# A pairwise-interaction tower: 31 couples of products added ahead of the sums, by GpSimd and by accumulating DMAs, with a longer ring and lag

## What is computed

```python
e = stack([tbl_f[ids[:, f]] for f in range(40)], axis=1)      # 512 x 40 x 64
viW = einsum('bpd,pde->bpe', e[:, i_idx, :], W)                # W: 780 x 64 x 64
z = einsum('bpe,bpe->bp', viW, e[:, j_idx, :])                 # 512 x 780
h = concatenate([z, dense_ctx], axis=1)                        # 512 x 796
h = maximum(h @ W_top1 + b_top1, 0)                            # 512
h = maximum(h @ W_top2 + b_top2, 0)                            # 256
y = h @ W_top3                                                 # 1
```

## Time and profile before

| | us |
|---|---|
| median of three runs | 349.21 |
| the profiled execution's own time | 349.04 |
| its span, first to last instruction | 346.9 |
| TensorE matmuls, busy | 329.1 (95%) |
| VectorE, busy | 249.6 (72%) |
| GpSimd, busy | 225.6 (65%) |
| ScalarE, busy | 22.1 (6%) |

### The profile page before, as it was taken

The page is one execution under the profiler, slowest core; times in us unless marked ns, Lnnn a source line. Parts: engine busy times, 40 slices in busy tenths (PEclk is TensorE's granted clock), DMA queues, the critical chain, the costliest instruction groups (busy, mean ns, idle before and its releaser), DMA issues.

```text
span 346.9 us, 4306 instructions
## 1 busy us (share of the span) xinstructions
PE 329.1 (95%) x1676; PEld 115.1 (33%) x1676; DVE 249.6 (72%) x248; ACT 22.1 (6%) x35; POOL 225.6 (65%) x191
## 2 busy tenths in 40 slices
PE   0799979899999999999999999999999999999997
PEld 0133333233333333333333333333333333333442
DVE  2484968778787888978889888988888898840000
ACT  1001100000000000000001000010000000000032
POOL 6777777777778889877788788576887423520000
PEclk9999989999999999999999999999999999999999
DMA  6984443243423238731322323232110000000000
GB/s 167 255 231 146 119 106 105 81 102 91 115 57 104 64 96 261 170 104 33 96 85 62 89 68 86 62 69 85 39 23 2 0 3 0 0 2 0 0 2 0
DMA packets 17854, 27.59 MB, mean 80 GB/s; under 512 B 4901, under 2 KB 5029, under 8 KB 17834
## 3 DMA queue, kind: packets, MB, share of 16 engines
q1 hardware_dynamic: 9770, 17.86, 17.7%
q0 software_dynamic: 4608, 4.73, 6.9%
q10 hardware_dynamic: 3456, 4.72, 4.8%
HBM read 22.57 MB, written 0.00 MB: 65 GB/s over the span
## 4 chain that ended last, share of the span: by engine, by line
PE 80%; POOL 13%; issue 4%; DMA 1%; ACT 0%
PE ps_t L421 47%; PE ps_z L443 21%; POOL rows L265 13%; PE ps_t L465 5%; PE ps_e L404 2%; PE ps_t L488 2%; PE ps_e L465 2%; DMA rows<-in_tbl,ids_sb 1%; DMA ids_sb<-in_ids_t 1%; PE ps_t L494 1%; ACT y_sb L328 0%
## 5 line engine op out<-in xcount | busy, mean ns | idle before, releaser
L372 DVE TENSOR_TENSOR prod<-ps_t,E 128x1024 f32<-128x1024 f32 x200 | 231.7, 1217 | 45.7 <-PE ps_t L421 44.9
L421 PE MATMUL ps_t<-E,w_sb 64*128 64x512 f32 x800 | 189.8, 609 | 0.8 <-ACT E L294 0.7
L265 POOL DMA_INDIRECT rows<-in_tbl,ids_sb x144 | 137.8, 957 | 43.4 <-issue 41.9
L272 POOL TENSOR_TENSOR prod<-prod 128x1024 f32<-128x1024 f32 x37 | 86.8, 2370 | 37.4 <-DVE prod L372 37.3
L421 PEld LDWEIGHTS ps_t<-E,w_sb 64*128 64x128 f32 x800 | 71.1, 187 | 109.6 <-issue 82.2
L443 PE MATMUL ps_z<-prod,quads 128*32 128x512 f32 x572 | 76.8, 600 | 0.0
L443 PEld LDWEIGHTS ps_z<-prod,quads 128*32 128x32 f32 x572 | 15.1, 109 | 48.9 <-DVE prod L372 29.1
L351 DVE TENSOR_SCALAR prod<-prod,first_row_f 125x512 f32<-125x512 int32 x38 | 16.6, 495 | 11.1 <-PE ps_e L395 5.1
L294 ACT ACTIVATE E<-ps_e 128x512 f32<-128x512 f32 x18 | 10.8, 598 | 192.4 <-PE ps_e L404 171.1
L395 PE MATMUL ps_e<-prod 125*64 125x512 f32 x40 | 12.1, 694 | 11.2 <-DVE prod L351 10.0
L465 PE MATMUL ps_t<-z,w_sb 128*128 128x512 f32 (+1 forms) x42 | 18.6, 595 | 0.0
(11 more groups left out here) (26 smaller groups left out, 21.1 us busy)
## 6 DMA issues: line engine op xcount, KB each, us to landing
w_sb<-in_w_units SPq DMA_DIRECT2D x50, 256.0 KB, 2.9
E<-E ACTq DMA_DIRECT2D x72, 64.0 KB, 2.3
rows<-in_tbl,ids_sb POOLq DMA_INDIRECT x144, 2.6
w_sb<-in_w SPq DMA_DIRECT2D x7, 256.0 KB, 4.5
prod<-in_ids_by_field SPq DMA_DIRECT2D x2, 512.0 KB, 9.0
prod<-in_tbl SPq DMA_DIRECT2D x3, 312.5 KB
w_sb<-in_w SPq DMA_DIRECT2D x1, 512.0 KB, 7.1
prod<-in_tbl SPq DMA_DIRECT2D x1, 250.0 KB
```

What stands on the lines that cost most here:

```text
L265: pool.indirect_dma_start(rows[:, g % G_RING, b, f * DIM:(f + 1) * DIM], None, tables[2 * k + f], bass.IndirectOffsetOnAxis(ap=ids_sb[:, c ...
L272: pool.tensor_tensor(prod[:, n % P_RING, 0, :, :], prod[:, n % P_RING, 0, :, :], prod[:, n % P_RING, 1, :, :], ALU.add).then_inc(halves_ad ...
L372: dve.tensor_tensor(prod[:, n % P_RING, s, :, :], ps_t[:, (2 * n + s) % STEPS, :, :], multiplier, ALU.mult).then_inc(product_ready, 1)
L421: last = pe.matmul(ps_t[:, step % STEPS, j, :], w_sb[at:at + DIM, m % W_RING, col:col + P], E[at:at + DIM, slot_of(pairs_of(n)[s][j]), :], ...
```

## The change

Three sizes change, the list of added groups is written out per couple, and half of the additions are made by DMAs that GpSimd issues. In the string a letter stands for each couple: P, GpSimd adds the halves of both groups itself; D, GpSimd issues for each of the two groups a DMA that adds the second half onto the first (`accum_op`); a dot, the couple is reduced in full. There are 15 P couples and 16 D couples.

```diff
-W_RING = 12
-P_RING = 8
+W_RING = 8
+P_RING = 12
-LAG = 7
+LAG = 11
-ADDED = [n for n, (_, M) in enumerate(GROUPS) if M is not None and n >= 20 and n // 2 % 2 == 1]
+ADDER = "........DPDP.PD.D.DPDP...DPPDPP.DPD.DPD..DPDPDPDP."
+ADDED_BY_POOL = [n for n in range(NG) if ADDER[n // 2] == "P"]
+ADDED_BY_DMA = [n for n in range(NG) if ADDER[n // 2] == "D"]
+ADDED = sorted(ADDED_BY_POOL + ADDED_BY_DMA)
-        E4 = sb("E4", [P, QUADS, 2, BATCH])
+        E4 = sb("E4", [P, QUADS - 1, 2, BATCH])
+        halves_added_by_dma = [sem(f"halves_added_by_dma{i}") for i in range(P_RING)]
             def add_halves(n):
                 pool.wait_ge(product_ready, 2 * n + 2)
+                if n in ADDED_BY_DMA:
+                    pool.dma_start(prod[:, n % P_RING, 0, :, :], prod[:, n % P_RING, 1, :, :],
+                                   accum_op=ALU.add).then_inc(halves_added_by_dma[n % P_RING], 16)
+                    return
                 pool.tensor_tensor(...)
...
                 for g in (n, n + 1):
                     pe.wait_ge(product_ready, 2 * g + 2)
-                    if g in ADDED:
-                        pe.wait_ge(halves_added, ADDED.index(g) + 1)
+                    if g in ADDED_BY_POOL:
+                        pe.wait_ge(halves_added, ADDED_BY_POOL.index(g) + 1)
+                    elif g in ADDED_BY_DMA:
+                        pe.wait_ge(halves_added_by_dma[g % P_RING],
+                                   16 * sum(a % P_RING == g % P_RING for a in ADDED_BY_DMA if a <= g))
...
-            reduce_two(NG - 6)
             pe.wait_ge(params_loaded, 16 * (CHUNKS + 5))
             pe.wait_ge(z_copied, CHUNKS - 2)
             pe.wait_ge(e_copied, KP)
             sum_h1(0, 0, CHUNKS - 2)
+            for n in range(NG - LAG + 1, NG - 4, 2):
+                reduce_two(n)
+            pe.wait_ge(product_ready, 2 * NG - 2)
+            sum_h1(1, 0, CHUNKS - 2)
+            sum_h1(2, 0, CHUNKS - 2)
             reduce_two(NG - 4)
-            sum_h1(0, CHUNKS - 2, CHUNKS - 1)
-            pe.wait_ge(product_ready, 2 * NG - 2)
-            sum_h1(1, 0, CHUNKS - 1)
             reduce_two(NG - 2)
-            for m in range(2, H1 // P):
-                sum_h1(m, 0, CHUNKS - 1)
+            sum_h1(3, 0, CHUNKS - 2)
+            for m in range(H1 // P):
+                sum_h1(m, CHUNKS - 2, CHUNKS - 1)
```

More of the change, by code:

```diff
@@ L300, in copy_fields @@
                         to, of = (2 * (k % 2) + f) * HALF, f * DIM + h * HALF
-                        act.dma_start(E4[to:to + HALF, k // 2, h, :], E[of:of + HALF, slot_of(k), :]).then_inc(
+                        act.dma_start(E4[to:to + HALF, k // 2 - 1, h, :], E[of:of + HALF, slot_of(k), :]).then_inc(
                             e4_placed[u], 16)
@@ L365, in multiply @@
                     if M is not None:
-                        multiplier = E4[:, M, s, None, :].to_broadcast([P, 2, BATCH])
+                        multiplier = E4[:, M - 1, s, None, :].to_broadcast([P, 2, BATCH])
                     elif s == 0:
```

## The result

The changed kernel takes 343.6 us (four runs, 342.95 to 345.45) against 349.6 (four runs): a ratio of 0.983, 95% interval 0.981 to 0.986. The forecast was 343.0. The profiled execution took 343.81, its span is 341.7.

A forecast was written before the change was run, and what follows sets the result against it. TensorE's work after 66.35 us was taken to bound the kernel: 349.04 less 8.6 gives 340.4, plus 2.6 for the late DMA of group 69 on GpSimd's queue gives 343.0 us; range 339.8 to 352.5.

The forecast's parts named there:

- TensorE's saving: Fully added couples rise from 17 to 31, 12.0 us less; two reductions uncovered by the lag, +3.4; net -8.6 us.
- the loop: Behind groups 11 to 97, ten more fully added couples: 8.6 us less by the products of group 99, 304.86 becoming 296.3.
- the tail: From the products of group 99 to the second layer: 31.06 us in the new order and in the old.
- What was to cost nothing: Product ring, weight ring and VectorE: no new wait, cost 0; bound of 6 us if VectorE's products were stretched to 1.217.
- GpSimd's queue as the next limit: GpSimd's in-order queue of gathers, adds and accumulating DMAs decides; it had no more than 0.31 us between any two entries.
- the term S: Lateness of group 69's accumulating DMA before the reduction of groups 68 and 69: 19c + l - 26.2, forecast 2.55 us.
- c: GpSimd's time to issue one accumulating DMA: taken as 1.25 us, bounded by 0.61 and 2.37.
- the ledger: Sum of GpSimd's queue entries up to group 69, whose DMA is issued at 219.9 + 19c.
- l: Time from an accumulating DMA's issue to its landing: taken as 5 us, ends 2.9 and 9.0.
- rival 1: Issue is cheap on GpSimd's queue: c up to 1.1, S at most 0, 340.4 us; chance 0.27.
- Rival 3: Slow landing of accumulating DMAs: c = 1.25 and l = 9 give S = 6.6 and 347.0 us; chance 0.10.
- my own sign: On TensorE: any wait in the first 66 us that is not there now would show the prediction wrong.

The follow-up runs named there:

- sizes-alone run: The changed kernel's rings of eight and twelve, LAG 11 and new end order, but the earlier 37 added groups, all by GpSimd: 353.32 us, 1.011 against the kernel before.
- the run with 36 couples: Changed kernel with parameters at u=8, first eight sums seven groups behind, and 36 couples added, 26 of them by DMA: 345.58 us, 0.987 against the kernel before.

## Why the prediction was right, and where it was not

**TensorE's saving: right.** 14 couples at 0.86, less two full reductions uncovered by the lag, -8.6 us net; the loop and the tail came out to 0.1 us once the two losses are added. The sizes-alone run confirms the lag's part by itself (3.45 for 3.4).

**What was to cost nothing: right.** VectorE's mean duration stayed (1217 to 1218 ns), and no wait on weights shows. VectorE's pace did show, 1.1 us, in the edits that left four groups without a sum between them.

**GpSimd's queue as the next limit: right as a mechanism**, shown by the run with all adds on GpSimd (14.4 us of waits for its rows and adds) and by the waits that came back when the first sums went early. That edit gained 1.8 us instead of 3.4: about 1.1 went to such waits, and about 1.1 to VectorE's pace (a little more than the 1.6 that are missing; the start was 0.2 earlier).

**The step that failed is the term S, its place and its size.** I put 2.55 us ahead of groups 68 and 69, and TensorE does not wait there at all. The issue cost less: I took c = 1.25; two issues take 1.98 to 2.25 (the first gathers behind an accumulating DMA are also longer, 1.07 and 1.00 instead of 0.94). The DMA for group 69 was issued at 241.71. GpSimd was by then 1.25 us behind the ledger for another reason (below), so the ledger gives 219.9 + 1.25 + 19c, and c = 1.08. The landing took 4.8, to 246.5, so l = 5 was right (by the slope that I used, reading twice would have been 5.3, not 4.9). With c = 1.08 and l = 4.8 the formula gives S = -0.9, which is nothing: rival 1 had that term right. TensorE came at 249.51 (the chain above); without the two other losses it would have come at 246.2, and the halves would have been added by 245.3. The Trainium skill ("DMA: Bandwidth & Descriptors", Specifications) states about 1 us for the software path's first byte. That is no price of an issue; read as one, as the prediction did for c = 1.0, it is nearer to the trace's 1.08 than my row is. In place of S stand two losses that I had not named: 1.36 us before group 11, and 1.98 at groups 28 and 29. Their sum, 3.3, is near the 2.6 that I had for another reason: 343.8 for 343.0 is partly luck.

**Why I missed the wait at groups 28 and 29.** Rival 3, slow landing, had the right mechanism, but as one l for the whole kernel; I looked at the DMA engines from 60 to 80 and 160 to 180 us, and not at 130 to 145, where the parameter loads stand. With the parameters moved away the wait was gone. The DMAs of SyncE, ScalarE and GpSimd run on the same engines, as the Trainium skill says ("DMA: Bandwidth & Descriptors", Issuing engines are not separate DMA queues); the trace agrees, 10.1 and 13.56 us for a pair of DMAs in the crowd against 5.4 and 7.5 for a pair outside it. A landing belongs to a stretch, as a wait does, and to a place in its row.

**Why I missed the 1.36 us.** I wrote that gathers had come at a spacing of 1.25 us since the start; the rows that I had read show it from 60 us on only. In GpSimd's timeline, first fence before, second after (start us, us), the first 24 gathers are not that regular:

```profile
33.39 0.94 POOL L265 DMA_INDIRECT rows<-in_tbl,ids_sb  x1 [0.30 <-issue]
```
```profile
20.67 1.25 POOL L270 DMA_INDIRECT rows<-in_tbl,ids_sb  x1 [0.31 <-issue]
...
34.65 0.94 POOL L270 DMA_INDIRECT rows<-in_tbl,ids_sb  x1 [0.31 <-issue]
...
64.60 0.94 POOL L270 DMA_INDIRECT rows<-in_tbl,ids_sb  x1 [0.30 <-issue]
```

Counted from the start, the 24th gather is issued at 33.39 before and at 34.65 after: eleven of them take over 1.1 us instead of six. From there on the spacing is the same, so the 48th, the last for the rows of u=7, stands at 63.35 before and at 64.60 after. Group 11 starts 3.0 and 3.1 us behind it. GpSimd is late, and not the landing, and the 1.25 us are most of the 1.36. Every traced run with the new sizes issued that gather later than the kernel before, by 0.3 to 1.3 us, those with the first sums early too; so the deferred sums are not the cause. All but the first of the slow gathers run beside VectorE's comparisons for the lookup (L360 in the changed kernel), but why more of them are slow stays open, and so does how much of it is chance: kernels that are alike up to there (the changed one, the one with earlier parameters, the one with all adds by GpSimd) issue the 48th at 64.60, 64.13 and 64.19, and of the kernel before one execution is traced. Without the first sums TensorE also waits 2.35 us for the rows of u=6, where it did not wait before: by my own sign, a wait in the first 66 us that was not there, that is a miss, though TensorE has to wait for u=7 afterwards all the same.

## What to carry to other kernels

Work taken off the bound engine counts in full only until the next engine's queue is late; price that queue entry by entry, with its order, up to each point where somebody waits for it. A DMA's landing is to be read in the stretch where it will run, beside the loads that already stand there, and several large ones in a row land one behind the other. A spacing read in one stretch need not hold in another: the pace of a queue is to be counted from its first entry. Deferring work past a point where its engine waits anyway turns free work into paid work.

## What the runs showed of the hardware

An accumulating DMA of 512 KB (SBUF onto SBUF, float32) cost GpSimd about 1.0 us and landed in 4.5 us at the least, 5.5 in the median of the changed kernel, 12.6 where 52 of them were used, 26.8 at worst. In a row they land one behind the other: 5.4 and 7.5 us for two, 20.64 for the last of six. After a wait of 2.96 us TensorE's granted clock was 0.57 and 0.58 over the stretches 130 to 134 and 134 to 138 us (part of them at 1.2 instead of 2.4 GHz); behind the 1.98 us wait of the changed kernel the products ran at their usual 1.92 us. The length of the last wait alone does not settle it: in the run with 36 couples the sum behind a wait of 3.09 us took its usual 1.06 in the timeline, the one behind a wait of 2.07 us 1.84. GpSimd's gathers took 0.94 us, and up to 1.28 in the first 30 us, beside VectorE's comparisons. GpSimd's adds beside an accumulating DMA's issue overlap in the records, so their mean of 2701 ns is not slower work: pairs of adds still take 4.69 to 4.72 us where no DMA issue stands ahead.
